# Attention's output projection leaves the attention stage and is fused with the layer norm that follows it

## The reference

```python
x = x + mamba(_layernorm(x))
x = x + ffn_top2(_layernorm(x))
x = x + attention(_layernorm(x))      # this change
x = x + ffn_experts(_layernorm(x))    # its layer norm: this change

def attention(x, Wqa, Wqb, Wkva, Wkvb, Wout, bout):    # 16 heads of 16, 4 key/value heads
    q = rope((x @ Wqa @ Wqb).reshape(b, s, 16, 16))
    k, v = split((x @ Wkva @ Wkvb).reshape(b, s, 4, 16, 2)); k = rope(k)
    w = softmax(where(causal, -inf, q @ k.T * scale))
    out = (w @ v).reshape(b, s, 256)
    return out @ Wout + bout

def _layernorm(x, eps=1e-5):
    return (x - mean(x)) / sqrt(var(x) + eps)
```

## Time and profile before

| | us |
|---|---|
| median of three runs | 2980.26 |
| the profiled execution | 2975.21 |
| its span | 2973.1 |
| TensorE busy (share of the span) | 2371.3 (80%) |
| VectorE busy | 1932.7 (65%) |
| ScalarE busy | 1025.0 (34%) |
| GpSimd busy | 1241.3 (42%) |

### The profile page before, as it was taken

How to read it: one execution, slowest core, us unless ns; L and a number is a source line. 1 busy time by engine, 2 the same in 40 slices (tenths; PEclk the granted TensorE clock), 3 DMA queues, 4 the chain that set the end, 5 groups by cost and what they waited for, 6 DMA issues and landing times. The chain is left out here.

```text
span 2973.1 us, 35670 instructions
## 1 busy us (share of the span) xinstructions
PE 2371.3 (80%) x10411; PEld 1252.0 (42%) x10413; DVE 1932.7 (65%) x2861; ACT 1025.0 (34%) x1511; POOL 1241.3 (42%) x696
## 2 busy tenths in 40 slices
PE   6984777778778775599966489999999624999998
PEld 3331223323323333376743124444443312766666
DVE  7897999999999995533326777777775454121110
ACT  4773333333333332022215225555555401111211
POOL 0347888898888890266632300000000001333332
PEclk9996899999889998699988669999999856999999
DMA  3557123033132104544432501111110112333322
GB/s 113 184 189 241 43 99 122 35 115 111 43 113 99 43 15 122 186 65 65 65 75 68 106 15 29 29 30 29 29 29 3 59 57 79 75 68 66 90 51 27
DMA packets 141565, 228.94 MB, mean 77 GB/s; under 512 B 25537, under 2 KB 89601, under 8 KB 141122
## 3 DMA queue, kind: packets, MB, share of 16 engines
q1 hardware_dynamic: 115314, 191.23, 20.6%
q0 software_dynamic: 26112, 35.96, 7.5%
HBM read 149.81 MB, written 77.34 MB: 76 GB/s over the span
## 5 line engine op out<-in xcount | busy, mean ns | idle before, releaser
L833 POOL TENSOR_TENSOR scan_hC<-scan_h,scan_c_all 128x1024 f32<-128x1024 f32 x256 | 612.3, 2404 | 105.7 <-DVE scan_h L762 105.1
L679 PE MATMUL banks<-scan_hC,all_ident 128*128 128x512 f32 x1024 | 535.7, 658 | 10.8 <-DVE scan_xc L769 8.9
L762 DVE TENSOR_TENSOR_SCAN scan_h<-scan_dA,banks 128x1024 f32<-128x1024 f32 x192 | 439.0, 2286 | 22.8 <-issue 3.0
L1805 ACT ACTIVATE attn_pt<-banks 128x256 f32<-128x256 f32 (+7 forms) x512 | 313.9, 651 | 333.6 <-PE banks L1733 329.9
L732 ACT ACTIVATE scan_dA<-scan_dt,mamba_a_neg 128x1024 f32<-128x1024 f32 x192 | 220.5, 1149 | 414.3 <-DVE scan_h L762 410.9
L1826 DVE TENSOR_REDUCE attn_m_lo<-banks 128x1 f32<-128x512 f32 (+3 forms) x512 | 288.0, 587 | 78.0 <-PE banks L1681 52.6
L669 PE MATMUL banks<-mamba_bc_parts,scan_pick 96*128 (+1 forms) x384 | 130.3, 425 | 222.8 <-DVE scan_h L762 197.9
L679 PEld LDWEIGHTS banks<-scan_hC,all_ident 128*128 128x128 f32 x1024 | 214.1, 211 | 219.2 <-issue 176.7
L1678 PE MATMUL banks<-attn_K,attn_Q 96*128 96x512 bf16 (+3 forms) x768 | 247.8, 357 | 44.9 <-DVE attn_mask L1818 27.4
L2295 DVE TENSOR_TENSOR ffn_y<-banks,ffn_gates 128x512 f32<-128x512 f32 x32 | 22.1, 692 | 359.1 <-PE banks L2194 352.4
L750 DVE TENSOR_TENSOR banks<-scan_du,banks 128x1024 f32<-128x1024 f32 x192 | 232.1, 1209 | 3.2 <-DMA scan_du<-scratch_du 3.2
(11 more groups left out here) (268 smaller groups left out, 3695.5 us busy)
## 6 DMA issues: line engine op xcount, KB each, us to landing
scan_c_all<-scratch_bc SPq DMA_DIRECT2D x64, 512.0 KB, 5.4
ffn_w<-in_e_w SPq DMA_DIRECT2D x16, 1024.0 KB
attn_Q<-scratch_q SPq DMA_DIRECT2D x96, 128.0 KB
scratch_x<-front_xc SPq DMA_DIRECT2D x8, 1024.0 KB
scratch_z<-front_zs SPq DMA_DIRECT2D x8, 1024.0 KB
scratch_dt<-front_lw SPq DMA_DIRECT2D x8, 1024.0 KB, 4.2
scratch_du<-front_du SPq DMA_DIRECT2D x8, 1024.0 KB
scan_dt<-scratch_dt SPq DMA_DIRECT2D x16, 512.0 KB, 4.8
```

The source lines that it names most:

```text
L679: mm = pe.matmul(PS[:, YB + i, :], ident[:, :], hC[:, s % NHC, i * BANK:(i + 1) * BANK], start=s == 0, stop=s == NST - 1, skip_group_check ...
L762: dve.tensor_tensor_scan(h[:, s % 2, :], decay, drive, 0.0, ALU.mult, ALU.add).then_inc(scanned, 1)
L833: pool.tensor_tensor(hC[:, s % NHC, :], h[:, s % 2, :], c_all[:, s, :], ALU.mult).then_inc(hC_done, 1)
L1805: act.activation(pt[:, kb % 2, j, 0:width], PS[:, SB_ + (j % 2) * 2:SB_ + (j % 2) * 2 + 2, :].rearrange("p a n -> p (a n)")[:, 0:width], A ...
```

## The change

1. The pieces `oT` and `proj` are gone from attention. `o_turn` writes the divided output to `o_all`, which holds all 32 tiles and lives on behind attention. Units (b+1,0) have the plan "mid", and `ending` has the two `o_turn` pieces only.
2. The hardware loops of attention are written out on all engines: 16 units in a straight line.
3. The output weight is no longer loaded by the stage before attention; SyncE loads it after the first maxima are sent, and waits for it at attention's end.
4. The bias is added to `X` in 32 instructions, one for each tile.
5. Stage "ln3" is replaced by `project_layernorm`: for each tile TensorE turns `o_all` (two transposes), ScalarE copies to `oT`, TensorE multiplies with the weight, VectorE adds to `X` and takes the statistics. From tile 20 on the normalised tiles of the first half are turned between the projections.

```diff
-PLANS = {"first": ..., "mid": ..., "out": unit_plan(True, True, True, True), "late": ..., "last": ...}
-ENDING = [("o_turn", 0), ("o_turn", 1)] + interleave_projection()
+ENDING = [("o_turn", 0), ("o_turn", 1)]
...
-            with fori(0, BATCH - 1) as b:
-                k = at
-                for kv in range(1, NKV):
-                    unit(b, kv, "mid", b * per_batch + k, k % 2)
-                    k += pieces_of("mid")
-                unit(b + 1, 0, "out", b * per_batch + k, k % 2)
-            at += (BATCH - 1) * per_batch
+            for b in range(BATCH - 1):
+                for nb, kv in [(b, kv) for kv in range(1, NKV)] + [(b + 1, 0)]:
+                    unit(nb, kv, "mid", at, at % 2)
+                    at += pieces_of("mid")
...
+            sp.dma_start(w_out[:, :, :], g["wout"].rearrange("(k p) c -> p k c", p=P)).then_inc(w_loaded, 16)
+            units(lambda w, k: None, unit, lambda k: None)
+            sp.wait_ge(w_loaded, 16)
...
-            pool.tensor_tensor(X[:, :, :], X[:, :, :], bout[:, None, :].to_broadcast([P, NT, DM]), ALU.add).then_inc(x_biased, 1)
-            with pool.Fori(0, BATCH - 1) as b:
+            for t in range(NT):
+                pool.tensor_tensor(X[:, t, :], X[:, t, :], bout[:, :], ALU.add).then_inc(x_biased, 1)
+            for b in range(BATCH - 1):
...
+def project_layernorm(nc, g, o_all, w_out, xnT, xn_all, rows_to, ahead):
...
+        HT, QT, PAIRS = NT // 2, NT // 4, NT // 2
+        OTB, OB = 4, 6
+        CHAIN = 9
+        BY_DVE = range(HT + 1, NT, 2)
+        ACT_PAIRS = tuple(range(PAIRS // 2 + 1, PAIRS, 2))
...
+        @block.sync
+        def _(sp):
+            for loads in ahead:
+                loads.start(sp)
+            dst = rows_to.rearrange("(t p) c -> p t c", p=P)
+            for i in range(4):
+                by_act, by_dve = made_by((i + 1) * QT)
+                sp.wait_ge(xn_act, by_act)
+                if by_dve:
+                    sp.wait_ge(xn_dve, by_dve)
+                sp.dma_start(dst[:, i * QT:(i + 1) * QT, :], xn_all[:, i * QT:(i + 1) * QT, :]).then_inc(rows_out, 16)
+            sp.wait_ge(rows_out, 64)
+        @block.tensor
+        def _(pe):
+            def turn_o(t):
+                if t >= 2:
+                    pe.wait_ge(oT_copied, t - 1)
+                for c in range(KC):
+                    mm = pe.transpose(PS[:, OTB + t % 2, c * P:(c + 1) * P], o_all[:, t, c * P:(c + 1) * P], ident[:, :])
+                mm.then_inc(oT_psum, 1)
+            def project(t):
+                pe.wait_ge(oT_copied, t + 1)
+                if t >= 2:
+                    pe.wait_ge(o_added, t - 1)
+                for c in range(KC):
+                    mm = pe.matmul(PS[:, OB + t % 2, 0:DM], oT[:, t % 2, c, :], w_out[:, c, :], start=c == 0, stop=c == KC - 1)
+                mm.then_inc(o_psum, 1)
+            def turn_xn(pair):
+                by_act, by_dve = made_by(2 * pair + 2)
+                pe.wait_ge(xn_act, by_act)
+                if by_dve:
+                    pe.wait_ge(xn_dve, by_dve)
+                if pair >= 4:
+                    if turned_by_dve(pair - 4):
+                        pe.wait_ge(turned_dve, count_dve(pair - 4))
+                    else:
+                        pe.wait_ge(turned_act, count_act(pair - 4))
+                for z in range(2):
+                    for k in range(KC):
+                        mm = pe.transpose(PS[:, pair % 4, (z * KC + k) * P:(z * KC + k + 1) * P],
+                                          xn_all[:, 2 * pair + z, k * P:(k + 1) * P], ident[:, :])
+                mm.then_inc(xnT_psum, 1)
+            turn_o(0)
+            for t in range(NT):
+                if t + 1 < NT:
+                    turn_o(t + 1)
+                project(t)
+                if t >= HT + 4 and t % 2:
+                    turn_xn((t - HT - 4) // 2)
+            for pair in range((NT - HT - 4) // 2, PAIRS):
+                turn_xn(pair)
+        @block.scalar
+        def _(act):
+            def copy_oT(t):
+                act.wait_ge(oT_psum, t + 1)
+                if t >= 2:
+                    act.wait_ge(o_psum, t - 1)
+                act.activation(oT[:, t % 2, :, :].rearrange("p c x -> p (c x)"), PS[:, OTB + t % 2, 0:KC * P],
+                               ACT.Copy).then_inc(oT_copied, 1)
+            def root(half):
+                at = slice(half * HT, (half + 1) * HT)
+                act.wait_ge(small, CHAIN * half + 7)
+                act.activation(rstd[:, at], var[:, at], ACT.Sqrt).then_inc(std_done, 1)
+            def normalise(t):
+                act.activation(xn_all[:, t, :], X[:, t, :], ACT.Identity, scale=rstd[:, t:t + 1],
+                               bias=nmr[:, t:t + 1]).then_inc(xn_act, 1)
+            for t in range(HT + 2):
+                copy_oT(t)
+            root(0)
+            act.wait_ge(small, CHAIN)
+            for t in range(HT + 2, NT):
+                normalise(t - HT - 2)
+                copy_oT(t)
+            for t in range(HT - 2, HT):
+                normalise(t)
+            root(1)
+            act.wait_ge(small, 2 * CHAIN)
+            for t in range(HT, NT):
+                if t not in BY_DVE:
+                    normalise(t)
+            for pair in ACT_PAIRS:
+                act.wait_ge(xnT_psum, pair + 1)
+                act.activation(turned(pair), banks(pair % 4), ACT.Copy).then_inc(turned_act, 1)
+        @block.vector
+        def _(dve):
+            def add_o(t):
+                dve.wait_ge(o_psum, t + 1)
+                dve.tensor_tensor(X[:, t, :], X[:, t, :], PS[:, OB + t % 2, 0:DM], ALU.add).then_inc(o_added, 1)
+            def count(t):
+                dve.wait_ge(o_added, t + 1)
+                dve.bn_stats(stats[:, t, :], X[:, t, :]).then_inc(stats_done, 1)
+            def chain(half):
+                at = slice(half * HT, (half + 1) * HT)
+                done = CHAIN * half
+                m0, v0, m1, v1 = (stats[:, at, i] for i in (1, 2, 4, 5))
+                dve.wait_ge(stats_done, (half + 1) * HT)
...
+            def finish(half):
+                at = slice(half * HT, (half + 1) * HT)
+                done = CHAIN * half
+                dve.wait_ge(std_done, half + 1)
+                dve.reciprocal(rstd[:, at], rstd[:, at]).then_inc(small, 1)
+                dve.wait_ge(small, done + 8)
+                dve.scalar_tensor_tensor(out=nmr[:, at], in0=mean[:, at], scalar=-1.0, in1=rstd[:, at],
+                                         op0=ALU.mult, op1=ALU.mult).then_inc(small, 1)
+            def copy_turned(pair):
+                dve.wait_ge(xnT_psum, pair + 1)
+                dve.tensor_copy(turned(pair), banks(pair % 4)).then_inc(turned_dve, 1)
+            for t in range(HT):
+                add_o(t)
+                if t:
+                    count(t - 1)
+            count(HT - 1)
+            chain(0)
+            add_o(HT)
+            add_o(HT + 1)
+            finish(0)
+            count(HT)
+            for t in range(HT + 2, NT):
+                add_o(t)
+                count(t - 1)
+                if t >= HT + 6 and t % 2 == 0:
+                    copy_turned((t - HT - 6) // 2)
+            count(NT - 1)
+            chain(1)
+            early = (NT - HT - 6) // 2
+            for pair in range(early, PAIRS // 2 - 1):
+                copy_turned(pair)
+            finish(1)
+            dve.wait_ge(small, 2 * CHAIN)
+            for t in BY_DVE:
+                dve.tensor_scalar(xn_all[:, t, :], X[:, t, :], rstd[:, t:t + 1], nmr[:, t:t + 1],
+                                  ALU.mult, ALU.add).then_inc(xn_dve, 1)
+            for pair in range(PAIRS // 2 - 1, PAIRS):
+                if turned_by_dve(pair):
+                    copy_turned(pair)
...
-            layernorm_transpose(nc, "ln3", g, xnT, xn_all, load_from=load_from, rows_to=xn_rows,
-                                ahead=(gate[-1], consts[-1]))
+            project_layernorm(nc, g, o_all, w_out, xnT, xn_all, xn_rows, ahead=(gate[-1], consts[-1]))
```

More of the change, by code:

```diff
@@ L1511, in bankful, with unit_plan @@
     return found
-def unit_plan(ahead, before, out, turn):
+def unit_plan(ahead, before, turn):
     assert len(MAXIMA) == sum(MAX_SHARE)
@@ L1527, in unit_plan @@
         plan[2][0:0] = [("o_turn", 0), ("o_turn", 1)]
[L1528 to L1534, removed]
-    return plan
-PLANS = {"first": unit_plan(True, False, False, True), "mid": unit_plan(True, True, False, True),
-         "out": unit_plan(True, True, True, True), "late": unit_plan(False, True, False, True),
-         "last": unit_plan(False, True, False, False)}
-ENDING = [("o_turn", 0), ("o_turn", 1)] + interleave_projection()
+    return plan
+PLANS = {"first": unit_plan(True, False, True), "mid": unit_plan(True, True, True),
+         "late": unit_plan(False, True, True), "last": unit_plan(False, True, False)}
+ENDING = [("o_turn", 0), ("o_turn", 1)]
 def pieces_of(kind):
@@ L1549, in attention_weights, with attention @@
```

(29 more changed lines are left out.)

69 lines of the change are left out of this document (43 added, 26 removed).

## The result

The changed kernel took 2937.9 us (median of 4 runs, 2934.4 to 2945.7) against 2980.0 for the kernel before: a ratio of 0.9862, 95% interval 0.9842 to 0.9883. 2943 was predicted, with 2930 to 2959 as the range. The profiled execution is 2934.4 us, its span 2932.6.

What follows compares the result with a forecast made beforehand. TensorE was taken to bound the middle of attention, busy 99.2 of 102 us. The terms -43.3 - 10.3 + 15.6 + 1 gave -37.0 us, so 2943 from 2980.26; own range 2934 to 2952, with rivals 2930 to 2959.

Steps and rivals of the forecast that it cites:

- Term 1: Attention's units: projection and loop turns leave, three "out" units become "mid" at 34.02 us, 43.3 us less.
- Term 2: Attention's start: bias in 32 pieces lets VectorE's two casts through early, loads are late next, 10.3 us less.
- Term 3: Attention's end and fused stage: 60.6 us in place of 45.0, 15.6 more, plus 1 for a slower-clocked gate stage.
- the tile: Fused stage: each tile takes TensorE 1.22 us, 0.86 for matrix instructions and up to 0.38 for transposes; 39.0 for 32.
- The break: Fused stage after tile 17: TensorE stands 2.7 us while ScalarE waits for VectorE's chain; 1.8 if the table is in.
- the start: Fused stage's beginning: first copy, and TensorE at half clock for a while, 1.5 us.
- The end at the landing of the last rows: Fused stage's end: last 1 MB of rows leaves at about 54.4 us, takes 4.6 to land, SyncE waits until 59.0.
- A: Attention's start: casts starve until GpSimd's last bias piece, 0 to 6 us later than before, total 2956; chance 12%.
- C: Written-out units: fetching code stalls TensorE 4.3 us a unit, 52 us over twelve, total 2995; 5% together with the hidden-projection rival.
- D: Attention's units: projection was hidden in gaps, so moving it is worth nothing; 5% together with the code-fetching rival.
- B: Fused stage stays serial at 1.65 us a tile, 14 us more, 2957, or at half clock, 2963; chance 11%.

Runs made afterwards that it cites:

- e6: Kernel before with only attention's loops written out, projection still in the units, bias one instruction: 2970.0 us, ratio 0.9979.
- e1: Changed kernel with attention's three turns as a hardware loop again on all engines: 2947.0 us, ratio 0.9905.
- e2: Changed kernel with the bias added by one GpSimd instruction again: 2946.8 us, ratio 0.9897.
- e3: Changed kernel with the bias in two GpSimd instructions of 16 tiles each: 2947.1 us (one run).
- e9: Changed kernel with one bias instruction again, but GpSimd starts it only after VectorE's three preparations: 2939.9 us, ratio 0.9879.
- e4: Kernel before with only the bias put in 32 GpSimd instructions: 2968.3 us, ratio 0.9973.
- e7: Changed kernel, but SyncE waits for the normalised rows' landing one stage later, in the stage that chooses the tokens: 2933.9 us, ratio 0.9860.
- e5: Changed kernel run again unaltered, as yardstick: 2940.9 us, 35.7 under the kernel before, ratio 0.9879.

## Why the prediction was right, step by step

- **Term 1** (-43.3 forecast, -40.8 measured). The three "out" units became "mid", and nothing else of the stage moved. Its parts are now known: the projection 3 x 10.78 = 32.3 us (e6), the two turns of the loop 50.84 - 45.02 and 49.43 - 45.02, together 10.2 us (e6; 5.0 and 5.6 in e1), less 9 x 0.21 = 1.9 us for the nine "mid" units, which are a little slower written out than looped; the third "out" unit gives the 0.1 that is left. The forecast took the pace as equal and put all twelve units at 34.02, and this is its error of 2.5 us (12 x 0.21); its bound was 0.25 us a unit. Unit (3,1), written out before already, could not show 0.2 us, since its interval ends in another plan. What costs the 0.21 us is open.
- **Term 2** (-10.3 forecast, -8.9 measured). The mechanism is shown by e2, e3 and e9, its worth alone by e4 (7.8 us). The 12 loads were late next, as said; from the first issue to TensorE it is 10.3 us and not the 9.0 that the sum gave (7.8 for the transfers and 1 for the semaphore).
- The rule of the Trainium skill (SBUF — State Buffer, Who interferes with whom) agrees with the traces in both halves: casts waited until the GpSimd instruction under way was through (rows of 5.88 us and 8.90 us in e3), and the reductions were not held back (62.3 us from the first max matmul to unit (0,0) in e9, 62.1 in the changed kernel). What the GPSIMD Engine Reference of the Trainium skill (Instruction dispatch) says against the change, that a core of GpSimd goes on to the next instruction by itself, did not keep VectorE out.
- **Term 3** (+15.6 and +1 forecast, +11.9 and +1.7 measured). The part that was mis-sized most is the tile: 1.22 us was taken, 1.08 measured, 4.3 us over 32 tiles, since the two transposes hold TensorE for 0.22 us and not for the 0.36 that I took from the length of their row. The break is 1.9 and not 2.7: the table load of 1.28 us ran while ScalarE waited for the chain anyway (2305.32, with the root at 2306.82), so the lower of my two values was right. Against these stands the start, taken at 1.5 us: the second and the third tile come 2.29 and 1.79 us behind the tile ahead of them, with the granted clock at the half level until 6.0 us behind the last division. With the 1.1 us from the first transpose to the first tile's matmuls the start took 3.0. The last projection ended 42.7 us behind the last division, where the forecast had 47.0. The end at the landing of the last rows was right (59.0 forecast from the stage's start, 55.4 measured); e7 shows it by taking it away. The gate stage did lose clock: its 32 matmuls took 5.34 us in place of 3.64.
- **The sum.** Forecast -37.0. From the first Q load to the store of `X`, without the first unit, the marks give -8.9 - 0.1 - 40.8 + 11.9 + 1.7 = -36.2. The first unit's 2.1 and 2.2 ahead of and behind these stretches, which come and go between executions, make it the -40.5 of the two spans. The terms' errors had both signs, and nearly cancelled: 2.5 and 1.4 us of gain too much, 3.0 of loss too much.
- **The three parts.** By the medians, the bias in pieces is worth 7.8 us (e4), the written-out loops 6.6 (e6), and the move of the projection 21.3 (e1 beside e4). They add up to 35.7, which is e5's gain (the loops' part was taken with the projection still in the units, and each median moves by some us, so the fit is better than it need be). So only some three fifths of the gain is the move of the projection; the two other parts can be had without it.
- **The rivals.** A is out by e3, C by e6 (what is left of it is at most the 0.21 us a unit, where it asked for 4.3), D by e6 (10.8 us a unit), and B by the pace of 1.08 us and by the granted clock of the stage, 0.92.
- **The median.** 2943 was forecast, 2937.9 measured, with 42.1 us between the two kernels there and 35.7 in e5. The forecast lies between them; it was no closer than the medians are steady.

## What to carry to other kernels

A long GpSimd instruction ahead of small VectorE casts is a wait for whoever needs the casts (a cast of 0.23 us took 14.50 here): put it behind them, or cut it small, but don't halve it, for in e3 the two engines took turns. Moving work out of an engine's full stretch into one where the engines wait for each other pays by the difference of what it costs the one and the other. Here 24 tiles left the full stretch at 1.35 us each (10.8 / 8), 32 us. The other grew by 11.9 us and the gate stage by 1.7, together 0.57 us for each of the 24, although a tile takes 1.08 us of TensorE there: the 8 tiles that it had before ran at 1.65, and statistics, normalising and turning now lie in part beside the projections. At the end of a stage, a wait for a store's landing that nobody in the next stage needs can move on.

## What was not expected of the hardware

Units written out in a straight line are 34.23 us long, the same in a hardware loop 34.02 to 34.04 (e1 beside e5), though TensorE's weight-load queue shows 9 sequencer rows in such a unit and not 75. Side by side, TensorE keeps step in the two traces for the first 22 us of a unit and loses the 0.2 us between there and 31. VectorE and GpSimd alternated by instruction even when GpSimd had the next one queued (e3). A turn of the loop leaves TensorE idle for 3.1 to 3.4 us behind "issue", and the clock is at the half level for 3.4 to 6.8 us from about there; whether it is the branch or the fetching of the code that takes this time was not tried.
